# Reciprocals spread over the partitions from a small DRAM buffer instead of from four SBUF rows

## The reference

```python
attn = softmax(q @ k.T)        # per head, 1024 x 1024
y    = attn @ v                # numerators, divided by the sums of the exponentials
out  = w_proj @ y + b_proj     # and a residual
```

## Time and profile before

| | |
|---|---|
| median of 3 runs | 482.24 us (482.12 to 482.79) |
| the profiled execution, its own time | 485.04 us |
| its span, first to last instruction | 483.3 us |
| busy: PE, VectorE (DVE), ScalarE (ACT), GpSimd (POOL) | 453.1, 362.8, 263.4, 214.4 us |
| mean granted clock of TensorE | 0.968 |
| `rec_sb<-den_sb`, on SP's queue | 9 DMAs of 256 KB |
| `den_sb<-rec_out`, on SP's queue | 9 DMAs of 8 KB |
| `SUMS<-SUMS`, on POOL's queue | 30 DMAs of 512 KB, median 5.7 us to landing |

### The profile page before, as it was taken

One profiled execution on the slowest core, in us unless ns is written; L12 is line 12 of the kernel. 1 busy time (PEld: TensorE's weight loads), 2 busy tenths in 40 slices (PEclk: granted clock), 3 DMA queues, 4 the chain that ended last, 5 costly groups with the idle time before them and its releaser, 6 DMA issues.

```text
span 483.3 us, 7009 instructions
## 1 busy us (share of the span) xinstructions
PE 453.1 (94%) x2210; PEld 239.1 (49%) x2210; DVE 362.8 (75%) x748; ACT 263.4 (54%) x515; POOL 214.4 (44%) x195
## 2 busy tenths in 40 slices
PE   8989999999896999999999799989999999979996
PEld 6544445553266575445444233657544544423463
DVE  7699888884777599987878356669997787817673
ACT  3238777775703237776757462224786677745032
POOL 8300031238010007897979811002799898960100
PEclk9979999999896999999999889999999999989999
DMA  5330544103300264679853520045388953551002
GB/s 154 56 64 21 156 69 125 22 8 62 61 6 1 60 147 100 154 155 195 189 105 57 104 48 21 1 109 126 72 176 166 191 102 70 98 100 26 0 1 87
DMA packets 20368, 41.87 MB, mean 87 GB/s; under 512 B 7170, under 2 KB 8458, under 8 KB 20076
## 3 DMA queue, kind: packets, MB, share of 16 engines
q1 hardware_dynamic: 15036, 25.41, 22.3%
q0 software_dynamic: 5152, 16.00, 17.9%
q10 hardware_dynamic: 144, 0.02, 0.0%
HBM read 5.94 MB, written 1.05 MB: 14 GB/s over the span
## 4 chain that ended last, share of the span: by engine, by line
PE 64%; DVE 10%; POOL 10%; DMA 4%; issue 4%; SPq 3%; ACT 3%; ACTq 0%; POOLq 0%; DVEq 0%
PE PV L1016 14%; PE S L977 13%; PE S L1005 13%; POOL SUMS L523 9%; DVE max L732 6%; DMA SUMS<-SUMS 3%; PE PV L929 3%; PE S L1140 3%; PE M L1029 3%; SPq L338 2%; PE PV L955 2%; PE S L1174 2%; PE M L955 2%; PE S L955 1%; SPq L331 1%
## 5 line engine op out<-in xcount | busy, mean ns | idle before, releaser
L732 DVE TENSOR_REDUCE max<-S 128x1 f32<-128x512 f32 x384 | 239.3, 683 | 39.7 <-PE S L977 38.7
L587 ACT ACTIVATE E<-S 128x512 f32<-128x512 f32 x384 | 206.5, 609 | 58.9 <-PE S L1005 53.3
L523 POOL TENSOR_TENSOR SUMS<-E 128x512 f32<-128x512 f32 x120 | 158.4, 1449 | 106.4 <-ACT E L587 102.0
L977 PE MATMUL S<-k_stack,q_stack 126*128 126x512 f32 x384 | 171.2, 460 | 5.8 <-DMA k_stack<-kL 3.4
L1005 PE MATMUL S<-q_stack,k_stack 128*128 128x512 f32 x384 | 156.0, 418 | 5.7 <-ACT E L587 5.2
L977 PEld LDWEIGHTS S<-k_stack,q_stack 126*128 126x128 f32 x384 | 72.9, 191 | 64.7 <-DVE max L732 35.4
L1005 PEld LDWEIGHTS S<-q_stack,k_stack 128*128 128x128 f32 x384 | 73.3, 193 | 38.3 <-ACT E L587 22.0
L1016 PE MATMUL PV<-E,V 128*32 128x512 f32 x768 | 92.0, 599 | 0.0
L1016 PEld LDWEIGHTS PV<-E,V 128*32 128x32 f32 x768 | 20.7, 110 | 46.9 <-issue 26.0
L498 POOL TENSOR_TENSOR att<-pv_sb,rec_sb 128x512 f32<-128x512 f32 x9 | 12.4, 1378 | 63.0 <-DMA rec_sb<-den_sb 63.0
L576 ACT ACTIVATE mHL<-S 8x128 fp32r<-8x128 f32 x48 | 12.7, 264 | 50.2 <-PE S L995 50.2
(11 more groups left out here) (175 smaller groups left out, 342.2 us busy)
## 6 DMA issues: line engine op xcount, KB each, us to landing
SUMS<-SUMS POOLq DMA_DIRECT2D x30, 512.0 KB, 5.7
k_stack<-kH SPq DMA_DIRECT2D x28, 128.0 KB, 2.3
q_stack<-qH SPq DMA_DIRECT2D x40, 64.0 KB, 2.0
rec_sb<-den_sb SPq DMA_DIRECT2D x9, 256.0 KB
q_stack<-qH SPq DMA_DIRECT2D x16, 128.0 KB, 2.8
k_stack<-kL SPq DMA_DIRECT2D x14, 128.0 KB, 4.1
k_stack<-kH SPq DMA_DIRECT2D x22, 64.0 KB, 2.3
q_stack<-qL SPq DMA_DIRECT2D x20, 64.0 KB, 2.0
```

The costliest lines, as they stand in the source:

```text
L523: pool.tensor_tensor(SUMS[:, slot, :], E[:, E_PLAN[s][0], :], E[:, E_PLAN[s + 1][0], :], ALU.add).then_inc(sum_ready, 1)
L587: act.activation(E[:, slot, :], B[:, ring_of_scores(s) % B_RING, :], ACT.Exp, scale=1.0 if l == 0 else float(HEAD_DIM[l]) ** -0.5).then_in ...
L732: dve.tensor_reduce(max8[:, m % 2, 2 * t + half:2 * t + half + 1], A[:, n % A_RING, :], AX.X, ALU.max).then_inc(a_used, 1)
L977: pe.matmul(A[:, n % A_RING, :], q_stack[0:SHIFT_ROW, slot, q0:q0 + P], k_stack[0:SHIFT_ROW, slot, k0:k0 + HALF], start=True, stop=True).t ...
```

## The change

A DRAM tensor `rec_rows` of 128 x 16 takes the reciprocals as they lie in `rec_out`; the spread reads it as 4 rows of 512 values. `den_sb` is no longer written by a DMA. The waits, the semaphores and the order of the queues are the same.

```diff
         QUARTER = HALF // 2
 
+        rec_rows = nc.dram_tensor("rec_rows", (P, PER_ROW), F32, kind="Internal").ap()
+
         block = ctx.enter_context(nc.Block())
...
             def reciprocal_rows(l, b):
 
                 sp.wait_ge(recs_folded, FOLDED * l + b + 1)
-                sp.dma_start(den_sb[0:P:DP, :].rearrange("u (d n) -> u d n", n=PER_ROW), rec_out[:, :]).then_inc(recs_rows, 16)
+                sp.dma_start(rec_rows, rec_out[:, :]).then_inc(recs_rows, 16)
 
             def spread_reciprocals(l, b):
...
                 sp.dma_start(rec_sb[:, :],
-                             den_sb[0:P:DP, :].rearrange("u (o n) -> u o n", o=1)
+                             rec_rows.rearrange("(u o d) n -> u o (d n)", u=HEADS_B, o=1)
                              .to_broadcast([HEADS_B, DP, HALF])).then_inc(recs_spread, 16)
```

## The result

The changed kernel takes 475.9 us (median of 4 runs, 475.46 to 476.86) against 482.51 (482.12 to 483.1, 4 runs): ratio 0.9865, 95% interval 0.9845 to 0.9884, 6.6 us faster. The forecast was 471.8 with a range of 470.0 to 481.0: the time is inside the range, 4.1 us above the forecast, and the saving is 3.8 us smaller than the 10.4 forecast. (The 482.51 has one run more, of 483.1, than the 482.24 that the forecast starts from.)

What follows compares the result with a forecast made beforehand. TensorE, busy 94% of the span, was taken to bound the kernel. Waits, slow clock and score matmuls summed to 5.7 us in layer 1 and 4.7 in layer 2, 10.4 in all: 471.8 us, range 470.0 to 481.0.

Steps and rivals of the forecast that it cites:

- The mechanism: Layers 1 and 2: a slow spread of rec_sb holds back unit 11's accumulate, which holds PE; total saving 10.4 us.
- the two waits at L1029: PE before block 2's denominators, waiting for unit 11's accumulate: 2.80 us in layer 1, 2.42 in layer 2; both go.
- the time beside the traffic: Latency part of the lone spread in layer 0: 6.99 us less 5.35 of traffic, 1.64 us, kept after the change.
- Unit 11's landing: Block 1, layers 1 and 2: its accumulate lands 7.6 and 8.3 us after issue, instead of 10.7 and 12.1.
- The rule that spoke against it: Spread: partitions 32 apart share a port, about 27 GB/s each; writes also 32 apart would keep 54 GB/s after the change.
- Rival 1: Spread: the writing side was the limit, so traffic stays near 5.35 us; about 482 us, chance 0.13.
- rival 3: Rows' landing in DRAM replaces what was saved, unit 11 slides; 1.4 us slower, about 483.6, chance 0.11.
- that case: Both PE waits before block 2's denominators gone: 471.8 us, own range 470 to 474.5, chance 0.65.
- the rival in which one of them stays: One of PE's two waits stays, or both in part: 477.5 us, range 475 to 480.5, chance 0.11.
- The saving is the same there.: Whole kernel: the 10.4 us saved on the profiled 485.04 also comes off the median of 482.24, giving 471.8.
- The four score matmuls behind L1029: PE, after block 2's denominators: would take some 1.15 us, saving 1.14 in layer 1 and 1.70 - 1.15 in layer 2.
- This chain: Rows, spread and normalise of block 2 at each layer's end: 2.4 us shorter, worth nothing since PE comes last.

Runs made afterwards that it cites:

- the later spread alone: Kernel before, with only the spread of block 1 issued behind unit 14's shift row instead of unit 13's, some 3 us later: 477.51 us.
- the other execution: The kernel before, unchanged, profiled once more: 482.54 us over 10 runs, the profiled one 482.52.
- the one with both repairs: Changed kernel, with block 1's normalise behind unit 12's accumulate instead of unit 13's, and block 2's normalise waiting for VectorE's adds: 475.7 us.
- the one with the moved normalise: Changed kernel, with POOL's normalise of block 1 behind unit 12's accumulate instead of unit 13's: 475.32 us.
- The run with POOL's added wait: Changed kernel with its DRAM spread split into four DMAs, plus block 2's normalise waiting for VectorE's 14 adds of the layer: 475.32 us.
- the kernel with four DMAs: Changed kernel, with the spread from DRAM as four DMAs, each one row to 32 partitions: 478.99 us.

## Why the prediction was right, and where it was off

**The mechanism held.** The spread was the cause, and the two waits at L1029 were the cost: the later spread alone removes them. Four engines stayed. The lone spread was forecast at 4.4 us and takes 5.0 (4.9 in block 0 of layer 0). From four SBUF ports it takes 4.55, so DRAM as a source adds up to 0.5 (0.3 in block 0 of layer 0, 0.2 at the end of layer 1). The traffic was sized right: 80, 102 and 86 GB/s, where 2.75 us for 256 KB are 95. Part of that is luck, as one of the two rows behind it, 283 GB/s "while one row is broadcast", is of a moment in which weights and head stacks were in flight too. What was short is the time beside the traffic, put at 1.64 us, which comes to some 2.2 (an estimate: 5.0 less 256 KB at about 90 GB/s). The rows' DMA was forecast at 2.0, bounds 1.8 to 2.5, and takes 1.40: the bound from below was too high, and the small write to DRAM takes less here than the one into four SBUF rows (1.82). These two misses of 0.6 us cancel, by luck. Unit 11's landing was forecast at 7.6 and 8.3 us and is 7.2 and 7.3. POOL's waits at block 0 went, and unit 11 goes out 2.2 us earlier in layer 1.

**The rule that spoke against it.** That the four source rows lie on two ports is borne out three times: 25 GB/s from one port, 49 from two, 96 to 102 from four. The Trainium skill's 27 GB/s a port (SBUF — State Buffer, Door 1) is near that. The part of my reading by which the writes would keep the old rate, as four engines write partitions 32 apart, didn't come true: the writes in the kernel with four ports are the old ones, and run at 96 to 102 GB/s. Rival 1 is out. So is rival 3, with 1.40 us for the rows.

**The size, 10.4 forecast and 6.6 measured.** Both waits went, and yet 475.9 lies outside the 470 to 474.5 given for that case; only the wider range, opened for the rival in which one of them stays, holds it. That the stated range was right is so in part luck. Two terms were mis-sized.

1. *"The saving is the same there."* The sum was made on an execution of 485.04 us and carried over to a median of 482.24. The profiled pair alone fits much better: the spans differ by 483.3 - 474.0 = 9.3. But most of what set that execution apart from the median lay in the very term that the change removes. In the other execution, which took 482.52 (span 480.8), the two waits are 1.78 + 2.34 = 4.1 us instead of 5.2. From the start of L1029 to the output projection it takes 20.3 us in layer 1 and 22.9 in layer 2, where the changed kernel has 20.0 in both. So the term is 4.1 + 0.3 + 2.8 = 7.2 us there, against 5.2 + 2.3 + 1.6 = 9.1 in the execution that the prediction read: 1.9 of the 2.5 us between the two spans. The 2.5 are this term's share of the miss.
2. *The four score matmuls behind L1029, 1.14 + 0.55.* In the profiled pair the stretch from L1029 to the output projection shrinks by 297.82 - 275.50 - 20.04 = 2.28 us in layer 1 and by 449.96 - 428.34 - 20.03 = 1.59 in layer 2. The matmuls of L1029 alone were forecast at 1.79 and 1.70, which leaves 0.5 and nothing for the score matmuls: 1.3 us of the miss. Windows of the changed kernel over the four score matmuls and from there to the output projection, then PE's timeline at the fourth:

```profile
274.31:276.01 1.70, 1.40 (x9) 0.67 (x12) 0.03 (x1) 1.15 (x3) 1.40 (x3) 1.00 0.00 0
276.01:292.50 16.49, 15.97 (x114) 5.75 (x113) 14.16 (x18) 9.48 (x18) 2.81 (x2) 1.00 0.23 50
422.48:424.17 1.69, 1.39 (x9) 0.67 (x12) 0.02 (x1) 1.14 (x3) 1.39 (x3) 1.00 0.00 0
...
275.51 0.50 PE L1007 MATMUL S<-q_stack,k_stack 128*128 128x512 f32 x1 [0.30 <-ACT E L589]
```

They take 1.70 us at full clock, not the 1.15 estimated, since the fourth waits for its exponential. The prediction had that number in its own rows: in layer 2 they took 1.70 at a clock of 1.00 already, so there was nothing to gain there, and in layer 1 only 2.29 - 1.70 = 0.59. That is 1.1 of the 1.3 us. The other 0.2 lies behind them, 16.49 us in each layer where it was 16.39 and 16.37. There the chain of the changed kernel, in order of time, runs through VectorE's adds to the last denominators, as the prediction hadn't named:

```profile
287.26 0.70 DVE SUMS L763
287.96 0.04 issue
288.00 1.06 PE M L1048 x8
```

The adds end just as TensorE needs them. That they are what costs the 0.1 us in each layer is argued, not shown.

**What I had costed at nothing.** "This chain gets 2.4 us shorter, which is worth nothing, since PE comes last." It is worth nothing only as long as the normalise doesn't come among VectorE's last adds. The changed kernel is at the edge of that: a spread that lands 1.6 us sooner still (3.3 us instead of 4.9 after its issue, end of layer 1) cost 3 us.

## What to carry to other kernels

Ask which ports lie under the few SBUF rows that a broadcast reads: here it ran at 25, 49 and about 100 GB/s from one, two and four of them. Moving the rows to other partitions may do what a detour through DRAM does, and here it gave the same 475.9 us. Look at what shares the DMA engines with a slow transfer: the wait that costs may be for another DMA altogether. Before carrying a saving over from a profile to a median, ask whether that execution's extra time lies in the very term being saved, and profile it once more.

## What the hardware showed beyond that

TensorE's clock: in the kernel before it stayed at 1.00 behind the wait of 1.78 us, and fell to 0.50 (1.2 instead of 2.4 GHz) for 3.4 to 6.9 us behind those of 2.34, 2.42 and 2.80. In layer 1, 1.0 us less of waiting came with 2.0 us less from L1029 to the output projection. But the length of the wait doesn't settle it. Two executions of different kernels, with the same pause of 0.77 us in layer 0 (the one with both repairs, then the one with the moved normalise), differ two microseconds and a half later:

```profile
124.25:127.60 3.35, 3.35 (x15) 1.15 (x19) 2.56 (x5) 2.38 (x5) 0.00 (x0) 0.50 0.18 26
```
```profile
124.25:127.60 3.35, 3.35 (x20) 1.07 (x21) 2.57 (x5) 2.28 (x5) 0.00 (x0) 1.00 0.17 26
```

VectorE and POOL hold each other up. An add of VectorE with both inputs in SBUF takes 0.69 us alone and 1.75 when POOL's normalise starts just ahead of it. The normalise takes 1.28 alone and 1.39 to 1.81 when it meets the last adds. (The 1.58 of a normalise right behind POOL's own DMA issue is another matter: it stands in the kernel before too, at 278.90, with no add beside it.) The Trainium skill (SBUF — State Buffer, SBUF: two separate sides) calls it an exclusive lock, held for a whole instruction, when VectorE has two inputs in SBUF and POOL reads SBUF. The trace agrees: the normalise ends at 275.59 + 1.58 = 277.17, and the add 0.56 us behind that. The run with POOL's added wait puts the price of such meetings at 3.7 us in the kernel with four DMAs.
